# Expert products moved across the slot border in an attention and mixture-of-experts kernel

## The reference

```python
x = x + xattn(layernorm(x), ctx)          # x: (2, 1024, 256), ctx: (2, 64, 256), 16 heads of 64
x = x + ffn(layernorm(x))

# ffn, over T = 2048 rows, E = 8 experts, C = T // E = 256 rows for each
norm = layer_norm(feat, ln_g, ln_b)
scores = norm @ centroids.T
for e in range(E):                        # balanced assignment
    s = where(taken, -inf, scores[:, e])
    idx = top_k(s, C); taken[idx] = True
routed = feat[sort_by_expert].reshape(E, C, D)
h = layer_norm(routed, ln_g, ln_b)
h = gelu(einsum('ecd,edf->ecf', h, w1) + b1)      # 256 -> 1024: the up product
h = einsum('ecf,efd->ecd', h, w2) + b2            # 1024 -> 256: the down product
out = routed + h, put back in the old order
```

## Time and profile before

| what | value |
|---|---|
| median of 3 runs | 344.44 us (343.03 to 345.68) |
| the profiled execution's own time | 346.77 us |
| its span, first to last instruction | 344.6 us |
| PE busy | 291.2 us (85%) |
| DVE, POOL, ACT busy | 219.5, 177.6, 144.7 us |
| mean granted TensorE clock | 0.93 of full speed |

### The profile page before, as it was taken

One profiled execution on the slowest core, in us unless ns is written; L12 is line 12 of the kernel. 1 busy time (PEld: TensorE's weight loads), 2 busy tenths in 40 slices (PEclk: granted clock), 3 DMA queues, 4 the chain that ended last, 5 costly groups with the idle time before them and its releaser, 6 DMA issues.

```text
span 344.6 us, 6499 instructions
## 1 busy us (share of the span) xinstructions
PE 291.2 (85%) x2066; PEld 256.0 (74%) x2066; DVE 219.5 (64%) x749; ACT 144.7 (42%) x265; POOL 177.6 (52%) x240
## 2 busy tenths in 40 slices
PE   8999799999999999998312379989989899899991
PEld 4999688989999899987201267777778687778890
DVE  0689898888878888784288666767676765120000
ACT  1466365455456554554400245353535353333320
POOL 8000533456665566545103655676767677885611
PEclk9999999999999999999655559999999999989997
DMA  7991006901000010001100232372718181806000
GB/s 275 346 390 26 2 0 245 363 34 64 30 30 30 30 61 30 30 33 61 61 0 0 66 120 61 81 257 64 274 43 289 35 288 42 314 2 210 34 11 20
DMA packets 21623, 37.50 MB, mean 109 GB/s; under 512 B 2400, under 2 KB 14944, under 8 KB 21216
## 3 DMA queue, kind: packets, MB, share of 16 engines
q1 hardware_dynamic: 19040, 30.89, 25.5%
q0 software_dynamic: 2560, 6.31, 6.0%
HBM read 30.90 MB, written 6.29 MB: 108 GB/s over the span
## 4 chain that ended last, share of the span: by engine, by line
PE 64%; DVE 13%; DMA 9%; issue 5%; POOL 5%; ACT 2%; DVEq 0%; POOLq 0%; ACTq 0%; SPq 0%
PE pair L886 55%; DMA G<-rows_scratch,idx 9%; PE pair L969 4%; DVE cmpb L750 3%; POOL G L414 2%; PE pair L936 2%; DVE pair L783 1%; POOL out_dram L445 1%; PE pair L1076 1%; PE pair L1041 1%; PE pair L998 1%; POOL w1p L424 1%; DVE wneg L600 1%; DVE G L790 1%; DVE ok L770 1%
## 5 line engine op out<-in xcount | busy, mean ns | idle before, releaser
L886 PE MATMUL pair<-w2s,hT 128*128 128x256 f32 x256 | 62.3, 394 | 0.0
L886 PE MATMUL pair<-yT,w1p 128*128 128x256 f32 x384 | 55.4, 297 | 0.0
L370 POOL TENSOR_TENSOR pr<-pr,rs 128x1024 f32<-128x1024 f32 x16 | 31.6, 1977 | 42.1 <-DVE rs L691 42.1
L886 PE MATMUL pair<-Bm,pT 128*128 (+1 forms) x384 | 50.0, 285 | 2.3 <-DVE pT L684 2.3
L886 PEld LDWEIGHTS pair<-w2s,hT 128*128 128x128 f32 x256 | 47.2, 195 | 6.2
L562 ACT ACTIVATE hT<-pair,b1s 128x256 f32<-128x256 f32 x64 | 26.8, 470 | 56.9 <-PE pair L886 56.6
L886 PEld LDWEIGHTS pair<-yT,w1p 128*128 128x128 f32 x384 | 50.2, 198 | 0.4
L886 PE MATMUL pair<-Am,xTp 128*128 (+1 forms) x192 | 48.7, 402 | 2.0 <-POOL xTp L358 2.0
L886 PEld LDWEIGHTS pair<-Bm,pT 128*128 128x128 f32 x384 | 47.0, 188 | 2.7 <-issue 2.7
L886 PEld LDWEIGHTS pair<-Am,xTp 128*128 128x128 f32 x192 | 34.9, 188 | 9.7 <-DVE Bm L594 2.4
L424 POOL TENSOR_TENSOR w1p<-w1s,w1p 128x512 fp32r<-128x512 f32 x32 | 40.0, 1274 | 0.2
(11 more groups left out here) (131 smaller groups left out, 525.1 us busy)
## 6 DMA issues: line engine op xcount, KB each, us to landing
w1s<-w_dram SPq DMA_DIRECT2D x8, 1024.0 KB
w2s<-w_dram SPq DMA_DIRECT2D x8, 1024.0 KB
rows_scratch<-row SPq DMA_DIRECT2D x16, 256.0 KB, 2.0
xs<-x_dram SPq DMA_DIRECT2D x1, 2048.0 KB, 17.1
xTs<-xT_dram SPq DMA_DIRECT2D x1, 2048.0 KB, 18.8
wk_s<-wk_dram SPq DMA_DIRECT2D x1, 1024.0 KB, 5.2
wv_s<-wv_dram SPq DMA_DIRECT2D x1, 1024.0 KB, 7.4
wqT_s<-wqT_dram SPq DMA_DIRECT2D x2, 512.0 KB, 8.8
```

What stands on the lines that cost most here:

```text
L370: pool_mul = nc.gpsimd.tensor_tensor(p4, p4, rs[:, v, :].unsqueeze(1).unsqueeze(3).to_broadcast([P, KG, H, K8]), ALU.mult)
L886: return nc.tensor.matmul(out_, l, r, start=start, stop=stop)
```

## The change

PE's table is changed so that the first four up blocks of an expert stand at the end of the slot in which its rows were gathered, and the last four at the start of the next slot; the down product follows in gaps 2 to 7 where it was in gaps 5 to 9 and gap 0 of the slot after. The list of an expert is made earlier: DVE does `slots`, `halves` and `Hoh` ahead of the first compare of the slot, `tokens` goes from gap 2 to gap 1, `spread` from gap 3 to gap 2, `indices` from round 3 to round 2. The two gathered halves are transposed in separate gaps (5 and 6). POOL does one part of `w1_rest` ahead of the gathers where it did two, and `y_rest` ahead of `bias`. ACT does the gelu of the first half of an expert at the end of the slot. SP issues the load of `w1` for expert e+1 ahead of that of `w2` for expert e. In slot 1 PE has three extra matmuls of 512 columns in each of six rounds (`keep_busy`), whose result nothing uses. `exp_r` is made in the preparation, and ACT makes the `xTp` copies of tiles 0 and 1 three fills earlier.

```diff
@@ SP
-            for e in range(2, E):
+            def load_w1(e):
                 v = e % 2
                 sp.wait_ge(e_w1l, W1_PARTS * (e - 1))
                 sp.dma_start(w1s[:, v], w1[e]...).then_inc(e_w1[v], 16)
+            load_w1(2)
+            for e in range(2, E):
+                v = e % 2
+                if e + 1 < E:
+                    load_w1(e + 1)
                 sp.wait_ge(e_o, ST * (e - 1))
                 sp.dma_start(w2s[:, v], w2[e]...).then_inc(e_w2[v], 16)
@@ ACT
+                if f == 20:
+                    act.wait_ge(s_in["cst"], 16)
+                    nc.scalar.activation(exp_r[:], expand, ACT.Copy).then_inc(r_init, 1)
+                if f == MIXED + 5:
+                    act.wait_ge(s_in["xT"], 16)
+                    for t in range(2):
+                        x_high(t, t)
...
-            nc.scalar.activation(exp_r[:], expand, ACT.Copy).then_inc(r_init, 1)
...
                 if 0 <= u < E:
                     rows(u, u % 2)
+                    for g in range(2):
+                        hidden(u, u % 2, g)
@@ DVE
+                if 0 <= u < E:
+                    slots(u)
+                    halves(u)
+                    one_hot(u, 1, Hoh, r_hoh)
                 for r in range(ROUNDS):
...
-                    if r == 0 and 0 <= k - 3 < E:
+                    if r == 0 and 0 <= u < E:
+                        one_hot(u, 0, Loh, r_loh)
+                    if r == 1 and 0 <= k - 3 < E:
                         final(k - 3, 1)
+                    if r == 3 and k == E - 1:
+                        select(k)
+                    if r == 2 and 0 <= u < E:
+                        indices(u)
-                    if r == 7 and 0 <= k - 2 < E:
+                    if r == 5 and 0 <= k - 2 < E:
                         final(k - 2, 0)
@@ PE
+            def keep_busy():
+                for _ in range(BUSY):
+                    mm(bank[1][:], ones_b[:, 0:P], ones_b[:], True, True)
...
-            UP = {1: (0, 2), 2: (2, 4), 3: (4, 6), 4: (6, 8)}
-            DOWN = {5: (0, 3), 6: (3, 6), 7: (6, 9), 8: (9, 12), 9: (12, 14)}
+            UP_FIRST = {8: (0, 2), 9: (2, 4)}
+            UP_REST = {0: (4, 6), 1: (6, 8)}
+            DOWN = {2: (0, 3), 3: (3, 6), 4: (6, 9), 5: (9, 12), 6: (12, 15), 7: (15, 16)}
...
+                    if 0 <= u < E:
+                        if r in (5, 6):
+                            rows(u, r - 5)
+                    if k == 1 and r >= 2:
+                        keep_busy()
```

More of the change, by code:

```diff
@@ L35 @@
 EPS = 1e-5
-WARM = 12
+WARM, BUSY = 12, 3
 TAKEN = -3.0e38
@@ L459, in _ @@
                     gather(e)
-                    w1_rest(e, v, 2)
-                    w1_rest(e, v, 3)
+                    for part in range(1, W1_PARTS):
+                        w1_rest(e, v, part)
+                    y_rest(e, v)
                     bias(e)
-                    y_rest(e, v)
             for i in range(GB * ST):
@@ L471, in mixed_high, with x_high @@
                 nc.scalar.activation(mixed(f, 0), fill_bank(f)[:], ACT.Copy).then_inc(s_evA, 1)
+            def x_high(t, v):
+                nc.scalar.activation(xTp[:, 0, v, :].rearrange("p (c n) -> p c n", c=CC), xTs[:, :, ds(t * P, P)],
+                                     ACT.Copy).then_inc(s_xTh, 1)
             def centre(h):
@@ L487, in _ @@
                     copy_fill(f, lambda to, src, scale: nc.scalar.activation(to, src, ACT.Copy, scale=scale)).then_inc(s_evA, 1)
-            act.wait_ge(s_in["xT"], 16)
             def attn(s, u):
                 t = s + 1
-                if live(t):
-                    v = par(t, u, -1)
+                if live(t) and not (isinstance(t, int) and t < 2):
                     wait(act, s_lg, t - 1)
-                    nc.scalar.activation(xTp[:, 0, v, :].rearrange("p (c n) -> p c n", c=CC), xTs[:, :, ds(t * P, P)],
-                                         ACT.Copy).then_inc(s_xTh, 1)
+                    x_high(t, par(t, u, -1))
                 t = s - 1
@@ L543, in rows @@
             def rows(e, v):
-                act.wait_ge(e_gT, e + 1)
+                act.wait_ge(e_gT, ST * (e + 1))
                 if e > 0:
@@ L569, in _ @@
                 act.wait_ge(s_row[v], 16 * T // 2)
-            nc.scalar.activation(exp_r[:], expand, ACT.Copy).then_inc(r_init, 1)
             for k in range(SLOTS):
                 e, u = k - 2, k - 1
-                for g in range(2):
+                for g in range(2, 4):
                     if 0 <= e < E:
@@ L1118, in expert_part @@
                 if 0 <= e < E:
-                    for f in range(*UP.get(gap, (0, 0))):
+                    for f in range(*UP_REST.get(gap, (0, 0))):
                         up(e, f)
@@ L1122, in expert_part @@
                         down(e, n)
-                if gap == 0 and 0 <= e - 1 < E:
-                    for n in range(14, 16):
-                        down(e - 1, n)
+                if 0 <= e + 1 < E:
+                    for f in range(*UP_FIRST.get(gap, (0, 0))):
+                        up(e + 1, f)
             spread_scores(0)
@@ L1131, in _ @@
                     expert_part(k, r)
+                    if 0 <= u < E:
+                        if r == 1:
+                            tokens(u)
+                        if r == 2:
+                            spread(u)
                     if searches(k):
@@ L1134, in _ @@
                     if 0 <= u < E:
-                        if r == 2:
-                            tokens(u)
-                        if r == 3:
-                            spread(u)
-                        if r == 6:
-                            rows(u)
-                    if r == 4 and k == E - 1:
+                        if r in (5, 6):
+                            rows(u, r - 5)
+                    if k == 1 and r >= 2:
+                        keep_busy()
+                    if r == 3 and k == E - 1:
                         ranks(k)
```

29 lines of the change are left out of this document (6 added, 23 removed).

## The result

| | before | changed |
|---|---|---|
| median of 12 runs each, side by side | 344.52 us (343.03 to 347.3) | 342.01 us (341.45 to 344.4) |
| the profiled execution's span | 344.6 us | 338.8 us |
| mean granted clock | 0.93 | 0.95 |

The ratio is 0.9926, 95% interval 0.990 to 0.9953: 2.5 us faster, where 5.5 was forecast. So the direction was right and the size less than half. Runs more than 1.5% above the fastest of their kernel are left out of all ratios.

The account below looks back on a forecast made before the run. PE was taken as the bound in full slots, DVE's serial search in slots 0 and 1. Terms of 8.85 us less, with 3.4 back for two clock falls, gave 5.5 less: 341.3 profiled, median 338.9, range 333.5 to 344.0.

Parts of the forecast that it names:

- exp_r early: Ahead of slot 0: PE no longer waits for `exp_r`, 3.3 us less, bounds 3.1 and 3.4.
- xTp early: First attention tile: PE's wait for `xTp` goes, 1.6 us less, bounds 0 and 2.0.
- Slot 1: 1.45 us more: Slot 1 now carries the first four up blocks: border at 17.0 instead of 15.55, bounds +0.5 and +4.
- A full slot in the new order: Walk through slots 3 to 5: 17.5 us each instead of 17.6, 2.3 idle in another place; 0.3 less together.
- The profiled execution would have 341.3: Whole kernel: 5.5 us less gives 341.3 profiled; the median of the runs, 2.3 below it, is 338.9.
- The tail: From the border of slot 6 to the last product: 61.3 against 65.1 us, 3.7 less, bounds -6 and 0.
- slot 2: Slot 2 becomes a full slot of 17.5 instead of 18.9 us, 1.4 less, bounds -2 and +1.5.
- the clock: Idle time of 2.3 us at each of eight crossings: two falls to half clock of 1.7 each, 3.4 us back.
- my sum ahead of the clock: Whole kernel: all terms before the clock's cost, 3.3 + 1.6 - 1.45 + 1.4 + 0.3 + 3.7 = 8.85 us less.
- rival 1: The clock holds at all crossings: 335.6 us, chance 0.28.
- Rivals 2 to 4: 2: nearly all crossings half-clocked, 349.2, 0.06; 3: gathers meet loads, 345.2, 0.10; 4: chain unbinding or slot 1 free, 331-333, 0.06.
- if the chain were covered after all, the slot would be 15.4 to 16: Full slot: bound for the case that other work covers the chain behind the transposes, 15.4 to 16 instead of 17.5 us.

Follow-up runs that it names:

- count-first kernel: Changed kernel with the count of round 1 ahead of the 16 token products on PE: median 339.19 us, ratio 0.9854.
- second series: Follow-up runs on another chip than the first and third series, each timed beside the kernel before, whose median there is 344.2 us.
- first and third series: Follow-up runs on one chip, each timed beside the kernel before, whose medians there are 342.1 to 342.9 us.
- crossings filled: Three extra matmuls in PE's wait at each crossing: added to the changed kernel 340.92 us, ratio 0.9905; to the count-first kernel 335.26 us, ratio 0.9788.
- old places: Changed kernel, products in their old gaps: 324.01 us (0.9449); with the count of round 1 ahead of token products 324.82; without slot 1's extra matmuls 328.07 (0.9525).

## Why the prediction was wrong

**"exp_r early" and "xTp early": right, 0.65 us too small.** The first border moved from 171.04 to 165.49. DVE starts to copy the masked scores at 165.04, 2.30 earlier, which is the part of `xTp` (forecast 1.6); the other 3.25 are `exp_r`'s (forecast 3.3). Of the 2.30, 1.78 show at DVE's first reduction (39.98, was 41.76) and 0.5 came in the attention behind, which I had kept at its length. Alone these copies are worth 5.8 us, more than twice the whole change.

**"Slot 1: 1.45 us more": 0.9 more**, within its bounds (16.45 against 15.55).

**"A full slot in the new order": the walk was right.** Slots with neither a late count nor a fallen clock take 17.3 to 17.5; 17.5 was forecast. The chain has its 2.3 and 3.2 us, PE's waits behind it are 0.43, 0.96 and 0.23, 1.6 in place of 2.3. The waits for gathers are gone. From the border of slot 6 to the end the count-first kernel needs 325.62 - 265.11 = 60.5, where the walk had 61.3.

**What these are set against: wrong, and this is the step that failed.** It stands in "The profiled execution would have 341.3, the median of the runs, which is 2.3 below it, 338.9". The changed kernel's profiled execution took 341.45 us, as forecast. But the median of its runs, 342.01, is not 2.3 below that; it is 0.6 above. I took the 2.3 us by which the profiled execution before lay above its median for an offset that both kernels share. From profile to profile the change gives 5.3 us, and 5.3 - 2.3 - 0.6 are the 2.5 of the medians.

Where that surplus sits is in part argued. The tail is the likely place: I priced the idle stretch of slot 7 and the half clock behind it (1.7 us) as a cost of every execution. The repeat of the same program has 1.49 us of idle and no half clock there, and its tail takes 62.1 us instead of 65.1. Among the 17 runs of the kernel before in the second series, nine have a mean clock of 0.939 to 0.941 and take 343.1 to 344.2 us, seven 0.935 to 0.937 and 344.8 to 345.8, and one 0.929 and 347.4; the execution that I read had 0.93. So a typical run has less time at half clock than the one I read, though the mean clock doesn't say in which slot. The late signals in slots 3 to 6 of that execution (52.9 us for slots 3 to 5 against 51.3 in the repeat) may go with the chip and stand in its other runs too.

**The hit of 341.3 was luck.** At the end of the last product the two profiles differ by 336.95 - 331.10 = 5.85 us; what follows is 0.5 us longer in the changed one. The preparation gave 0.65 more than forecast, slot 1 0.55, slot 2 0.2, the tail 0.5, the clock 0.6, and slots 3 to 5, without late counts and half clock, 0.4: together 2.9 us too pessimistic. Two late counts, which the sum has at nothing, took 2.6 of it back.

**What the new slots give by themselves** is seen best on the one chip of the first and third series, between the repeat of the kernel before and the kernel with the count first, neither of whose profiles has a late count, or half clock in the slots from slot 3 on. There the new order gives 5.5 (preparation) - 1.1 (slot 1, 15.40 to 16.51) + 0.4 (slot 2) - 0.9 (slots 3 to 5, 51.3 to 52.2) + 1.6 (tail), 5.5 us in all, where my sum ahead of the clock had 8.85. All of it is the preparation; the new slots give nothing in these profiles, and no more than the 1.3 us above with the crossings filled.

**"The clock": mechanism and place right.** The clock fell at two of eight crossings in one profile of the changed kernel, and at one in the other. A slot with a fall is longer by 1.2 (slot 3 without the extra matmuls, 18.6) to 2.0 us (slot 2 of the second execution, 19.4); I had 1.7. In both profiles with the wait filled the clock holds.

**Late counts: a term put at nothing.** The walk has `tokens to 3.8` and the three down steps behind it, and never asked when DVE sees the count between them. In two slots of the first profile (3 and 5), and in three of the second (4 to 6), that is 1.8 us after it starts. In the kernel before a late signal delays the list, and its slots 3 to 5 are 0.5 us longer each than in the repeat, where none is late; in the new order DVE's search is nearly as long as the slot, and 1.3 us reach the border. The changed kernel's profiled execution lost 2 x 1.3 so and 2 x 1.4 to the clock, 5.4 in all: 331.10 at its last product against 325.62 in the undisturbed profile with the count first.

**The rivals.** With the wait filled and the count first the ratio is 0.9788 (0.9743 to 0.9833), where rival 1's 335.6 stands for 0.974; it took two further edits to get there. Rivals 2 to 4 did not happen.

**What I didn't ask** is which half of the change removes the 2.4 us. The early lists do it without the split, with the rest of the edit in place (15.53 us a slot). The walk had the figure, "if the chain were covered after all, the slot would be 15.4 to 16", and I used it as a bound without seeing that the other half of the edit is what uncovers the chain.

**Open:** why a count behind sixteen small matmuls is seen late in some slots and not in others, why in six profiles and in none of the eight of one chip, whether moving it ahead helps where it is late, and whether the extra matmuls of slot 1 favour it.

## What to carry to other kernels

Where the profiled execution lies above the median of the runs, its surplus may sit in the very stretches that a change shortens and is then no offset: take the base of a comparison from more than one execution, and compare one chip with itself. Before a cure is tried, see that the trouble shows in the same setting without the cure: the run with the count first was made where no count was late anyway. Asking when each engine sees each signal belongs in a walk; here a late count was worth 1.3 us a slot. And before steps are moved across a border, name the chain that they cover where they are: here ten down steps covered 3.2 us in every slot. Moving them costs 10.4 us beside the old places on the chip without late counts (335.26 against 324.82), and 14 on the other (0.9936 against 0.9525).

## What the runs showed of the hardware

- The kernel before took 340.95 to 346.9 us in one series on one chip, and 343.1 to 347.4 in another series on another chip. The profile from the result's chip (span 344.6) shows token products that ACT has 1.3 to 2.0 us after their start in slots 3 to 6, where 0.7 is usual, and a clock that fell in slot 7; the repeat (338.8) shows neither. In the changed kernel DVE has a count 1.8 us late, just after the end of the block behind it, where 0.2 to 0.3 is usual. Such late signals are in all six profiles of the result and the second series and in none of the eight of the other chip.
- The granted clock fell to 1.2 GHz after an idle stretch of 2.01 us in slot 7, and behind some crossings with waits of 0.43, 0.96 and 0.23 us close together, but not after 1.49 us in the repeat, nor after 1.99 at the attention's start. With extra matmuls in the crossing (0.59 us in the profile) it held at 2.4 GHz in both profiles that have them.
- In the old places one group of extra matmuls at the end of slot 1 went with a clock of 1.00 from 194 to 198, where it was 0.58 without it; slot 2 was 1.3 us shorter than in old places and 2.4 shorter than in the kernel that differs by this group alone.
